# Block-scaled MLP's down projection as three float32r products, one step later; order of maxima and x in grouped attention

## The reference

```python
def _mx_dequant(t):
    blocks = t.reshape(rows, feat // 32, 32)
    max_abs = jnp.max(jnp.abs(blocks), axis=-1)
    scales = jnp.maximum(max_abs / 448.0, 1e-30)
    q = (blocks / scales[..., None]).astype(jnp.float8_e4m3fn).astype(jnp.float32)
    return (q * scales[..., None]).reshape(rows, feat)

def _mx_linear(x2d, w):
    return _mx_dequant(x2d) @ _mx_dequant(w).T
# mlp: g = _mx_linear(h, gate_w); u = _mx_linear(h, up_w)      (256 -> 1024)
#      y = _mx_linear(silu(g) * u, down_w)                     (1024 -> 256)
# x = x + y, h = layernorm(x)
```

## Time and profile before

| | us |
|---|---|
| median of 3 runs | 1566.57 (1566.49 to 1571.78) |
| the profiled execution | 1572.63 |
| its span, first to last instruction | 1570.6 |
| busy TensorE (share of the span) | 1484.7 (95%) |
| busy weight loads on TensorE | 1211.0 (77%) |
| busy VectorE | 1072.1 (68%) |
| busy ScalarE | 967.5 (62%) |
| busy GpSimd | 726.9 (46%) |
| mean granted TensorE clock | 0.984 of full speed |

### The profile page before, as it was taken

How to read it: one execution, slowest core, us unless ns; L and a number is a source line. 1 busy time by engine, 2 the same in 40 slices (tenths; PEclk the granted TensorE clock), 3 DMA queues, 4 the chain that set the end, 5 groups by cost and what they waited for, 6 DMA issues and landing times. The chain is left out here.

```text
span 1570.6 us, 30305 instructions
## 1 busy us (share of the span) xinstructions
PE 1484.7 (95%) x10256; PEld 1211.0 (77%) x10256; DVE 1072.1 (68%) x2474; ACT 967.5 (62%) x2612; POOL 726.9 (46%) x892
## 2 busy tenths in 40 slices
PE   6999979999999999899997999899999999989998
PEld 2666668888888888788874454389999999967887
DVE  4676657888888887654445777655656665588887
ACT  2667647777777777532325777567777777742222
POOL 3666625555555555232333333213444344447675
PEclk8999989999999999999998999999999999999999
DMA  6000020000000000000002000020000000000000
GB/s 245 2 1 1 2 97 5 3 5 3 5 3 4 3 3 1 22 1 1 1 33 102 1 2 1 1 105 8 8 8 8 1 8 5 1 1 14 10 15 17
DMA packets 15609, 29.82 MB, mean 19 GB/s; under 512 B 1505, under 2 KB 12002, under 8 KB 14690
## 3 DMA queue, kind: packets, MB, share of 16 engines
q1 hardware_dynamic: 15458, 27.89, 4.9%
HBM read 25.79 MB, written 2.10 MB: 18 GB/s over the span
## 5 line engine op out<-in xcount | busy, mean ns | idle before, releaser
L1453 POOL TENSOR_TENSOR weights_even<-weights_even,cross_reciprocal 128x512 f32<-128x512 f32 x64 | 66.6, 1041 | 202.6 <-DVE cross_reciprocal L1684 202.6
L935 POOL TENSOR_TENSOR cross_work<-cross_work,cross_reciprocal 128x512 f32<-128x512 f32 x64 | 66.6, 1040 | 174.5 <-DVE cross_reciprocal L1092 174.5
L1535 ACT ACTIVATE weights_even<-bank,cross_shift 128x128 f32<-128x128 f32 x256 | 90.5, 365 | 80.0 <-DVE cross_shift L1676 80.0
L1158 PE MATMUL bank<-ident,cross_work 128*128 128x128 f32 x768 | 117.6, 276 | 2.5 <-DVE cross_work L1070 2.2
L988 ACT ACTIVATE cross_work<-bank,cross_shift,cross_q_rms 128x128 f32<-128x128 f32 x256 | 113.6, 455 | 5.3 <-DVE cross_shift L1064 4.5
L1158 PEld LDWEIGHTS bank<-ident,cross_work 128*128 128x128 f32 x768 | 90.1, 141 | 30.1 <-DVE cross_work L1070 21.2
L2476 DVE TENSOR_REDUCE grouped_maxima<-bank 128x4 bf16<-128x512 f32 x128 | 82.2, 684 | 34.8 <-PE bank L2558 34.8
L1960 POOL TENSOR_TENSOR mlp_low_inner<-mlp_inner,mlp_high_inner 128x512 fp32r<-128x512 f32 x36 | 48.7, 1354 | 116.4 <-ACT mlp_high_inner L2003 116.4
L1674 DVE TENSOR_REDUCE cross_maxima<-bank 128x4 f32<-128x512 f32 x64 | 44.2, 690 | 83.6 <-PE bank L1816 83.6
L405 POOL TENSOR_TENSOR causal_masked_maxima<-causal_maxima,causal_constants 128x512 bf16<-128x512 bf16 x64 | 67.0, 1068 | 56.7 <-DVE causal_maxima L550 56.7
L2824 ACT ACTIVATE mx_silu<-bank 128x512 f32<-128x512 f32 x32 | 19.1, 598 | 113.4 <-PE bank L2974 113.3
(11 more groups left out here) (375 smaller groups left out, 5295.0 us busy)
## 6 DMA issues: line engine op xcount, KB each, us to landing
weights_even<-in_weights SPq DMA_DIRECT2D x2, 2560.0 KB, 11.6
weights_even<-in_weights SPq DMA_DIRECT2D x2, 1732.0 KB, 8.8
weights_odd_early<-in_weights SPq DMA_DIRECT2D x1, 3072.0 KB, 12.0
weights_odd_values<-in_weights SPq DMA_DIRECT2D x1, 3072.0 KB, 19.0
weights_odd_late<-in_weights SPq DMA_DIRECT2D x2, 1536.0 KB, 9.8
x<-in_x SPq DMA_DIRECT2D x4, 512.0 KB, 7.7
out<-mx_result SPq DMA_DIRECT2D x16, 128.0 KB, 1.7
weights_even<-in_weights SPq DMA_DIRECT2D x2, 512.0 KB, 5.5
```

The costliest lines, as they stand in the source:

```text
L935: pool.tensor_tensor(probs[x], probs[x], reciprocal[x][:, :].unsqueeze(2).to_broadcast([P, PER, P]), ALU.mult).then_inc(probs_divided, 1)
L1158: last = pe.transpose(bank[:, j * P:(j + 1) * P], source, core.ident[:, :])
L1453: pool.tensor_tensor(probs[x], probs[x], reciprocal[x][:, :].unsqueeze(2).to_broadcast([P, JOBS, P]), ALU.mult).then_inc(probs_divided, 1)
L1535: last = act.activation(probs[x][:, j, :], bank_scores[x][:, j * P:(j + 1) * P], ACT.Exp, scale=SCALE, bias=shift[x][:, j:j + 1], accum_ou ...
```

## The change

The down projection is done in float32r like the others: `copy_innerT` writes the high half of the inner activations, VectorE subtracts it from the bank for the low half, the down weights are split once after step 1, and `down` adds three products. It is moved one step later, between the two projections of a step; the last batch keeps its float32 path. In grouped attention the first pair's maxima go ahead of `update_x`, and GpSimd's `add_bias` ahead of the narrowing. The block scale and the cross attention's shift become `scalar_tensor_tensor` instructions, with the constant as a tensor in SBUF.

```diff
@@ dve_block_scale, used by every dve_scale
-    return dve.tensor_scalar(scratch.scale[:, :], scratch.largest[:, :], core.scale_bounds[:, 0:1],
-                             core.scale_bounds[:, 1:2], ALU.mult, ALU.max)
+    return dve.scalar_tensor_tensor(scratch.scale[:, :], scratch.largest[:, :], 1.0 / FP8_MAX,
+                                    core.least_scale[:, 0:1].to_broadcast([P, scratch.blocks]), ALU.mult, ALU.max)
@@ masked_cross_attention, VectorE
+            dve.memset(minus_scale[:, :], -SCALE).then_inc(minus_scale_ready, 1)
+            dve.wait_ge(minus_scale_ready, 1)
...
-                dve.tensor_scalar(shift[x][:, :], maxima[x][:, :], LEAST_MAX, -SCALE, ALU.max, ALU.mult)\
+                dve.scalar_tensor_tensor(shift[x][:, :], maxima[x][:, :], LEAST_MAX, minus_scale[:, :], ALU.max, ALU.mult)\
@@ grouped_attention, GpSimd
                 if batch_there(t + 1):
+                    if t + 1 > 0:
+                        add_bias(t + 1)
                     narrow_q(t + 1, 1 - s)
                     narrow_own_keys(t + 1, 1 - s)
-                    add_bias(t + 1)
+                    if t + 1 == 0:
+                        add_bias(t + 1)
@@ mx_mlp, ScalarE
+            def copy_high_down():
+                act.wait_ge(weights_ready, WEIGHT_JOBS - TURNED_EARLY)
+                for m in range(0, TILES, 2):
+                    act.activation(down_split[0][:, m:m + 2, :], w_down[:, m:m + 2, :], ACT.Copy).then_inc(down_high, 1)
...
+                if isinstance(t, int) and t == 1:
+                    copy_high_down()
@@ mx_mlp, VectorE
+            def make_low_down():
+                for k in range(WEIGHT_JOBS - GATE_UP_JOBS):
+                    dve.wait_ge(down_high, k + 1)
+                    dve.tensor_tensor(down_split[1][:, 2 * k:2 * k + 2, :].rearrange("p i n -> p (i n)"),
+                                      w_down[:, 2 * k:2 * k + 2, :].rearrange("p i n -> p (i n)"),
+                                      down_split[0][:, 2 * k:2 * k + 2, :].rearrange("p i n -> p (i n)").bitcast(F32),
+                                      ALU.subtract).then_inc(down_low, 1)
+
+            def make_low_innerT(b, j):
+                dve.wait_ge(innerT_ready, HALVES * b + j + 1)
+                dve.tensor_tensor(innerT[1][:, 4 * j:4 * j + 4, :], bank_turn[j].rearrange("p (i t) -> p i t", i=4),
+                                  innerT[0][:, 4 * j:4 * j + 4, :].bitcast(F32), ALU.subtract).then_inc(innerT_low, 1)
...
+                if isinstance(t, int) and t == 1:
+                    make_low_down()
@@ mx_mlp, TensorE
+                        pe.wait_ge(innerT_low, HALVES * b + m // 4 + 1)
+                    for x, y in PARTS:
+                        last = pe.matmul(bank_y[:, 0:EMBED], innerT[x][:, m, :], down_split[y][:, m, :],
+                                         start=(m == 0 and (x, y) == PARTS[0]),
+                                         stop=(m == TILES - 1 and (x, y) == PARTS[-1]))
...
                     if batch_there(t - 1):
                         project(t - 1, j)
+                    if j == 0 and batch_there(t - 3) and t - 3 != VERY_LAST:
+                        down(t - 3)
                     if batch_there(t - 2):
                         turn_inner(t - 2, s, j)
...
                     turn_h(t)
-                if batch_there(t - 2):
-                    down(t - 2)
```

More of the change, by code:

```diff
@@ L249, in _ @@
             pool.memset(core.ones_bf[:, :], 1.0)
-            pool.memset(core.scale_bounds[:, 0:1], 1.0 / FP8_MAX)
-            pool.memset(core.scale_bounds[:, 1:2], LEAST_SCALE)
+            pool.memset(core.least_scale[:, :], LEAST_SCALE)
             pool.memset(core.ones[:, :], 1.0).then_inc(made, 1)
@@ L1369, in masked_cross_attention @@
         scratch = [Scratch(layer, f"weights{k}", SLICE) for k in range(2)]
+        minus_scale, minus_scale_ready = sbuf("minus_scale", [P, JOBS]), sem("minus_scale_ready")
         normed = sbuf("normed", [P, BOTH * EMBED])
@@ L2527, in step @@
                     normalise_heads(t - 1)
+                if batch_there(t + 1):
+                    row_maxima(t + 1, 1 - s, 0, 0)
                 if batch_there(t - 2):
@@ L2722, in mx_mlp @@
         inner_q = [sbuf(f"inner_q{s}", [P, INTER]) for s in range(2)]
-        innerT = sbuf("innerT", [P, TILES, P])
+        last_innerT = sbuf("last_innerT", [P, TILES, P])
+        innerT = [sbuf(f"{half}_innerT", [P, TILES, P], F32R) for half in ("high", "low")]
+        down_split = [sbuf(f"{half}_down", [P, TILES, EMBED], F32R) for half in ("high", "low")]
         result = [sbuf(f"result{s}", [P, EMBED]) for s in range(2)]
@@ L2736, in mx_mlp @@
         half_filled, silu_ready, inner_ready = sem("half_filled"), sem("silu_ready"), sem("inner_ready")
-        innerT_filled, innerT_ready = sem("innerT_filled"), sem("innerT_ready")
+        innerT_filled, innerT_ready, innerT_low = sem("innerT_filled"), sem("innerT_ready"), sem("innerT_low")
+        down_high, down_low = sem("down_high"), sem("down_low")
         last_chain, last_rounded = sem("last_chain"), sem("last_rounded")
@@ L2828, in copy_innerT @@
                 act.wait_ge(layer.y_filled, nonneg(b))
-                act.activation(innerT[:, 4 * j:4 * j + 4, :], bank_turn[j].rearrange("p (i t) -> p i t", i=4),
+                place = last_innerT if b == VERY_LAST else innerT[0]
+                act.activation(place[:, 4 * j:4 * j + 4, :], bank_turn[j].rearrange("p (i t) -> p i t", i=4),
                                ACT.Copy).then_inc(innerT_ready, 1)
@@ L2840, in copy_last_piece @@
                 first = TILES // HALVES + TILES_A_PIECE * k
-                act.activation(innerT[:, first:first + TILES_A_PIECE, :],
+                act.activation(last_innerT[:, first:first + TILES_A_PIECE, :],
                                last_banks[k][:, 0:PIECE].rearrange("p (i t) -> p i t", t=P),
@@ L2929, in step @@
                                              core.rstd[:, LEFT_BY_PAIR:], ALU.mult, ALU.mult).then_inc(shift_ready, 1)
-                if batch_there(t - 3) and t - 3 != VERY_LAST - 1:
-                    add_to_x(t - 3, 1 - s)
                 if late(t) is not None:
@@ L2940, in step @@
                             make_low(t)
+                        if j == 1 and batch_there(t - 2):
+                            make_low_innerT(t - 2, j)
                         scale_inner(i, j)
+                        if j == 0 and batch_there(t - 2):
+                            make_low_innerT(t - 2, j)
+                        if j == 0 and batch_there(t - 3):
+                            add_to_x(t - 3, 1 - s)
                     if t - 1 == VERY_LAST:
@@ L2946, in step @@
                     make_low(t)
+                if t - 3 == VERY_LAST:
+                    add_to_x(t - 3, 1 - s)
+                if isinstance(t, int) and t == 1:
+                    make_low_down()
             batches(dve, step)
@@ L2979, in turn_inner @@
                 pe.wait_ge(inner_rounded, HALVES * b + j + 1)
-                pe.wait_ge(innerT_ready, nonneg(HALVES * (b - 1) + j + 1))
+                pe.wait_ge(innerT_low, nonneg(HALVES * (b - 1) + j + 1))
                 for m in range(4 * j, 4 * j + 4):
@@ L2996, in down @@
                     if m % 4 == 0:
-                        pe.wait_ge(innerT_ready, HALVES * b + m // 4 + 1)
-                    last = pe.matmul(bank_y[:, 0:EMBED], innerT[:, m, :], w_down[:, m, :],
-                                     start=(m == 0), stop=(m == TILES - 1))
+                        pe.wait_ge(innerT_low, HALVES * b + m // 4 + 1)
[3 more added lines that the diff above has]
+                                         stop=(m == TILES - 1 and (x, y) == PARTS[-1]))
                 last.then_inc(layer.y_filled, 1)
@@ L3003, in down_tiles @@
                 for m in tiles:
-                    last = pe.matmul(bank_y[:, 0:EMBED], innerT[:, m, :], w_down[:, m, :],
+                    last = pe.matmul(bank_y[:, 0:EMBED], last_innerT[:, m, :], w_down[:, m, :],
                                      start=(m == 0), stop=(m == TILES - 1))
@@ L3016, in turn_piece @@
                     pe.wait_ge(last_rounded, k + 1)
+                    pe.wait_ge(innerT_low, HALVES * VERY_LAST)
                     for i, m in enumerate(tiles_of(k)):
@@ L3041, in step @@
                         project(t - 1, j)
+                    if j == 0 and batch_there(t - 3) and t - 3 != VERY_LAST:
+                        if isinstance(t, int) and t == 3:
+                            pe.wait_ge(down_low, WEIGHT_JOBS - GATE_UP_JOBS)
+                        down(t - 3)
                     if batch_there(t - 2):
@@ L3049, in step @@
                     turn_weights((6, 7))
-                if batch_there(t - 2):
-                    if isinstance(t, int) and t == 2:
-                        pe.wait_ge(weights_ready, WEIGHT_JOBS - TURNED_EARLY)
-                    down(t - 2)
             batches(pe, step)
```

3 lines of the change are left out of this document (1 added, 2 removed).

## The result

The changed kernel takes 1584.65 us (median of 4 runs, 1580.35 to 1585.09), the kernel before 1569.17 beside it (4 runs, 1566.49 to 1572.31): 1.0084 of before, interval 1.0066 to 1.0102. It is slower: the ratio makes it 13.2 us, while the two medians lie 15.5 apart. The forecast was +13.3, and 1580 us in all. The profiled execution took 1585.09 us (span 1582.9), 12.3 more span than before. The starts of one and the same matmul in both traces say where.

What follows compares the result with a forecast made beforehand. The prediction took TensorE to bound the steady block-scaled MLP at 10.29 us a step. Its terms, 11.3 + 6 + 3 - 7 + 0 = +13.3 us on the median 1566.57, gave 1579.9, say 1580 us, range 1568.5 to 1589.5.

Steps and rivals of the forecast that it cites:

- Steady MLP: Block-scaled MLP, batch 4 to 15: the path to low hT lies open, a step takes 11.3 us against 10.29; +11.3 us.
- T+2.1: When TensorE goes on in a steady MLP step, 2.1 us after T, the second projection's issue.
- So 0.22 + 23 x 0.12 = 3.0 us: Predicted time of the down projection's 24 float32r products in an MLP step, against 3.27 us in float32.
- rival B: VectorE becomes the bound in the MLP, a step of 12.1 us; +8.8 on top, 1588 us; chance 0.12.
- Early steps: MLP until batch 4: four down-weight subtractions (3.9) and queued inner subtractions (2.1) delay TensorE; +6 us (2.8 to 7).
- End: End of the MLP: batch 13's down projection +3.0, batch 14's low half +0.7, a rounding wait -0.7; +3.0 us (2.3 to 3.7).
- Scale and shift: Block scale and cross attention's shift: the new form, with two SBUF operands, still contends with GpSimd; 0 us.
- rival A: The new scale and shift don't wait for GpSimd: -7.8, so +5.5 in all, 1572 us; chance 0.16.
- Grouped attention: Maxima ahead of the addition to x begin 0.49 us earlier, about 0.5 in each of 14 waits; -7.0 us (0 to -9.8).
- Rival C: Grouped attention gives nothing, as the later addition to x holds up the transposes of h; +20, 1587 us; chance 0.11.

Runs made afterwards that it cites:

- float32_late: The changed kernel with the down projection in float32 again (8 products, no low halves of inner activations or down weights), at its new place; 1585.78 us, 1.0087 of before.
- cover_sum_first: The changed kernel with batch t-3's down projection behind the transposes of h, split inner activations buffered twice, addition to x starting VectorE's step; 1576.9 us, 1.0048 of before.
- old_scale: The changed kernel with the block scale and the cross attention's shift as tensor_scalar again; 1584.8 us, 1.0094 of before.
- old_place: The changed kernel with batch t-2's three float32r products behind the transposes of h, VectorE's second inner low half before low hT; 1593.18 us, 1.0157 of before.
- no_low_down: The changed kernel without the four subtractions for the down weights' low half, the high half used instead, same number of products; 1579.3 us, 1.0062 of before.
- grouped_only: The kernel before with only the two grouped-attention moves (maxima ahead of the addition to x, bias addition ahead of the narrowing); 1572.41 us, 1.0002 of before.
- filler: The kernel before with both grouped-attention moves and twelve unread matmuls in TensorE's waits in that stage's last three steps; 1563.87 us, 0.9964 of before.
- cover: The changed kernel with batch t-3's down projection behind the transposes of h, split inner activations buffered twice, addition to x behind the first half's scaling; 1598.46 us, 1.0171.

## Why the prediction was right, and where by luck

- *Steady MLP*, +11.3 forecast, +9.5 measured: the mechanism, its place (T+2.1 against T+2.14) and its releaser were right. That VectorE would be through with the gating product was a guess, and it was so by 0.03 us (1504.78 against the high half's 1504.81). The size was off in "So 0.22 + 23 x 0.12 = 3.0 us", which measured 2.86: 0.14 too much in each of eleven steps, 1.5 of the 1.8. float32_late and cover_sum_first show it to be the place, not VectorE: rival B is out.
- *Early steps*, +6 forecast, +5.9 measured, but of other parts: 2.9 for the four subtractions (3.9 forecast), at least 1.7 with the rest of the splitting (2.1 forecast, for the inner subtractions), and at most 1.35 with the new place, which costs in these steps too and had no term there. Nor had the clock, which falls with the longer wait (0.90 and 0.84). That the sum fits is luck in part.
- *End*, +3.0 forecast, +1.9 measured. float32_late has the same end, 21.7 us, without any low half; it was not taken apart further.
- *Scale and shift*, 0 forecast, 0 measured by old_scale; rival A is out. The rule that the prediction weighed here, from the Trainium skill's page "SBUF — State Buffer", section "Who interferes with whom" (a VectorE instruction with two SBUF inputs contends with a GpSimd instruction that reads SBUF), agrees with the maximum of 1033 ns and with the four subtractions, 5.53 us.
- *Grouped attention*, -7.0 forecast. The stall went as described, in twelve steps by 0.47 where I had counted fourteen by 0.5: -5.6. What failed is the step from the stage to the kernel: I took TensorE's clock as given. In the change's profile 4.2 us come back at the handover. Rival C had the right outcome, that the edit alone gives nothing (1.0002), by the wrong mechanism: the later addition to x holds nobody up.
- The -3.3 us ahead of grouped attention lies in stages that the change doesn't touch, and goes with the clock: the cross attention ahead of the gated MLP took 445.46 us at 0.99 in before's profile and 441.12 at 1.00 in the change's. Without it the span would have grown by 15.6, and the medians did differ by 15.5; that the total came so near is partly luck: an unforeseen loss of 4.2 at the handover and an unforeseen gain of 3.3 nearly cancel.

What stays open: in other profiles with the same grouped code (old_scale, cover_sum_first, old_place, no_low_down) the handover took 51.9 to 52.7 us, so the clock gives back 0.4 to 4.2 us from one kernel's profile to another. What decides between these, and why before goes through the same waits at full clock, no run here shows. In grouped_only's one profile handover and end together give back 5.9 us; where its other runs lost the gain isn't on record.

## What to carry to other kernels

When an instruction is moved, ask first what it had been hiding: here 3.3 us of TensorE's work between the transposes and the next projection hid a wait that is now 1.3 us a step, and the cheaper products save only 0.4. A sum that frees a bank belongs where it is ready, not where its stage stands in the list. Where a faster stage saves nothing, compare the granted clock and the same matmuls' times behind it; here a few matmuls in TensorE's waits at the handover kept the gain (0.9964 against 1.0002 of before), and alone they cost nothing that could be measured (1.0007).

## What was new of the hardware

- The clock was granted at half (1.2 GHz) where TensorE's longest single wait was 1.66 us (grouped_only, 991.63 to 1047.40 at 0.88), in a stretch that before went through with the same waits, 6.6 us later in its span, at 1.00. With twelve matmuls more in these waits it was 1.00 (filler). With one wait of up to 1.9 us in each of eleven steps it was 0.95 (cover), with one of 1.3 it was 1.00 (the change).
- Four VectorE subtractions with both operands in SBUF took 5.53 us in all beside GpSimd, 0.68 the first and 1.53 to 1.78 the others, and a GpSimd addition beside them took 1.67 instead of 1.29; the cost falls on both.
- A VectorE instruction of 128x16 elements took 293 ns at the least as `tensor_scalar` with both constants as per-partition scalars, and 174 as `scalar_tensor_tensor` with one constant in the instruction and the other as a tensor in SBUF; GpSimd was idle beside the shortest ones.
